# Softmax over 2048 keys with a maximum for each half: one running maximum replaced by two local ones in an attention kernel

## What is computed

```python
logits = jnp.einsum('bhid,bhjd->bhij', q, k) * SCALE
logits = jnp.einsum('bhij,gh->bgij', logits, Wpre)
attn = jax.nn.softmax(logits, axis=-1)
attn = jnp.einsum('bhij,gh->bgij', attn, Wpost)
out = jnp.einsum('bhij,bhjd->bhid', attn, v)
```

## Time and profile before

| | us |
|---|---|
| median of 3 runs | 9106.78 (9100.24 to 9108.23) |
| the profiled execution, its own time | 9105.46 |
| its span in the trace | 9103.7 |
| TensorE busy | 8367.6 (92%) |
| VectorE busy | 8179.9 (90%) |
| ScalarE busy | 7239.7 (80%) |
| GpSimd busy | 5882.0 (65%) |

### The profile page before, as it was taken

The page is one execution under the profiler, slowest core; times in us unless marked ns, Lnnn a source line. Parts: engine busy times, 40 slices in busy tenths (PEclk is TensorE's granted clock), DMA queues, the critical chain, the costliest instruction groups (busy, mean ns, idle before and its releaser), DMA issues.

```text
span 9103.7 us, 399510 instructions
## 1 busy us (share of the span) xinstructions
PE 8367.6 (92%) x158060; PEld 4657.2 (51%) x158060; DVE 8179.9 (90%) x12269; ACT 7239.7 (80%) x13696; POOL 5882.0 (65%) x12005
## 2 busy tenths in 40 slices
PE   7999999997799999999779999999977999999997
PEld 3555555554455555555445555555544555555554
DVE  7999999996899999999689999999968999999996
ACT  5888888885588888888558888888845888888884
POOL 5666666663566676667356667666636666766663
PEclk9999999998899999999889999999989999999998
DMA  0000000002000000000100000000020000000002
GB/s 30 7 8 9 8 8 8 9 8 68 21 7 8 8 9 7 8 8 9 67 21 8 8 8 9 8 8 8 9 67 21 8 8 8 9 8 8 8 9 76
DMA packets 100978, 143.32 MB, mean 16 GB/s; under 512 B 8097, under 2 KB 90657, under 8 KB 96801
## 3 DMA queue, kind: packets, MB, share of 16 engines
q1 hardware_dynamic: 99104, 117.57, 3.9%
HBM read 75.60 MB, written 41.94 MB: 13 GB/s over the span
## 4 chain that ended last, share of the span: by engine, by line
DVE 43%; PE 32%; issue 19%; DVEq 2%; ACT 1%; SPq 1%; DMA 1%; POOL 0%; POOLq 0%; ACTq 0%
PE psS L1172 16%; DVE top L814 14%; DVE big L828 13%; DVE pl L854 9%; PE psP L1192 6%; PE psO L1207 6%; PE psM L1218 1%; DVE top L820 1%; ACT big L642 1%; DVE rr L846 1%; PE psS L1305 1%; PE psS L1147 1%; PE psS L1334 1%; DVEq L813 0%; DMA d_ct<-cT 0%
## 5 line engine op out<-in xcount | busy, mean ns | idle before, releaser
L828 DVE SCALAR_TENSOR_TENSOR big<-psP,big 128x512 f16<-128x512 f32 x4096 | 2608.7, 676 | 289.8 <-ACT big L642 280.7
L814 DVE TENSOR_REDUCE top<-psS 128x1 f32<-128x1024 f32 x2048 | 2482.5, 1212 | 224.1 <-PE psS L1172 223.7
L642 ACT ACTIVATE big<-psP 128x512 f16<-128x512 f32 x4096 | 2199.5, 589 | 581.9 <-PE psP L1192 576.0
L1172 PE MATMUL psS<-KH,AH 128*128 128x512 f16 x8192 | 2466.1, 383 | 81.8 <-POOL AL L440 80.0
L1172 PE MATMUL psS<-KH,AL 128*128 128x512 f16 x8192 | 2441.9, 380 | 0.0
L1172 PE MATMUL psS<-KL,AH 128*128 128x512 f16 x8192 | 2441.3, 380 | 0.0
L624 ACT ACTIVATE pr<-psS,nb 128x1024 f32<-128x1024 f32 x2048 | 2281.4, 1114 | 69.9 <-ACT nb L611 3.9
L652 ACT ACTIVATE ph<-pr 128x1024 f16<-128x1024 f32 x2048 | 2151.8, 1051 | 32.3
L1192 PEld LDWEIGHTS psP<-rh,ph 64*128 64x128 f16 x32768 | 1433.9, 95 | 1221.8 <-DVE big L828 1037.8
L1192 PE MATMUL psP<-rh,ph 64*128 64x64 f16 x32768 | 1682.6, 192 | 383.0 <-DVE big L828 345.6
L854 DVE TENSOR_TENSOR pl<-pr,ph 128x1024 f16<-128x1024 f32 (+1 forms) x2048 | 2024.3, 988 | 0.0
(11 more groups left out here) (138 smaller groups left out, 8004.7 us busy)
## 6 DMA issues: line engine op xcount, KB each, us to landing
ph<-in_xT SPq DMA_DIRECT2D x16, 512.0 KB, 4.4
xr<-in_x SPq DMA_DIRECT2D x64, 128.0 KB, 2.1
d_x<-x SPq DMA_DIRECT2D x64, 128.0 KB, 1.7
d_xn<-xn SPq DMA_DIRECT2D x64, 128.0 KB, 1.7
d_lg<-lg SPq DMA_DIRECT2D x64, 128.0 KB, 1.7
d_ct<-cT SPq DMA_DIRECT2D x64, 128.0 KB, 1.7
Q<-in_w SPq DMA_DIRECT2D x8, 1024.0 KB, 12.2
out<-V SPq DMA_DIRECT2D x16, 512.0 KB, 3.3
```

Source lines behind the costliest of these rows:

```text
L642: a.activation(PT[:, hf * JH:(hf + 1) * JH, :, 0, i0:i0 + HQ], psP[:, ih, :].rearrange("p (j g i) -> p j g i", j=JH, g=H), ACT.Copy, scale ...
L814: v.tensor_reduce(top[:, t % 2, h:h + 1], psS[:, 2 * h:2 * h + 2, :].rearrange("p c n -> p (c n)"), X, ALU.max).then_inc(s_mx, 1)
L828: v.scalar_tensor_tensor(out=PT[:, js, :, 1, i0:i0 + HQ], in0=psP[:, ih, :].rearrange("p (j g i) -> p j g i", j=JH, g=H), scalar=MDROP, in ...
L1172: mm = pe.matmul(psS[:, c, :], A_[:, k8, k, :], K_[:, k, c * CW:(c + 1) * CW], start=n == 0, stop=n == 5)
```

## The change

Each half is now exponentiated with its own maximum, so half 1 no longer needs the maximum of half 0. `row_bound` is gone from VectorE. GpSimd works out nm, the smaller of the two negated maxima (`lower_bound`); ScalarE makes two factors from it, ff = exp(nm - nb) for each half, in the place where it made f0; GpSimd weighs both sums with them (ws), adds them (tot), and after VectorE's reciprocal (now rc) multiplies both factors by it (rr). On GpSimd, `total` also stands behind `mixq` now, with `lower_bound` in its old place.

```diff
+                def lower_bound(T, t):
+                    p = t % 2
+                    g.wait_ge(s_nb, T * 2 + 2 + 1)
+                    apart(g)
+                    g.tensor_scalar(nm[:, p:p + 1], nb[:, p, 0:1], nb[:, p, 1:2], None, ALU.min).then_inc(s_nm, 1)
...
                 def total(T, t):
                     g.wait_ge(s_exp, T * 2 + 2 + 1)
                     g.wait_ge(s_f, T + 1 + 1)
-                    g.tensor_scalar(tot[:, p:p + 1], sums[:, p, 0:1], f0[:, p:p + 1], sums[:, p, 1:2],
-                                    ALU.mult, ALU.add).then_inc(s_tot, 1)
-                def first_half(T, t):
+                    g.tensor_tensor(ws[:, p, :], sums[:, p, :], ff[:, p, :], ALU.mult).then_inc(s_ws, 1)
+                    g.wait_ge(s_ws, T + 1 + 1)
+                    g.tensor_tensor(tot[:, p:p + 1], ws[:, p, 0:1], ws[:, p, 1:2], ALU.add).then_inc(s_tot, 1)
+                def weights(T, t):
                     g.wait_ge(s_rec, T + 1 + 1)
-                    g.tensor_tensor(rr[:, p, 0:1], rr[:, p, 1:2], f0[:, p:p + 1], ALU.mult).then_inc(s_r0, 1)
+                    g.tensor_tensor(rr[:, p, :], ff[:, p, :], rc[:, p:p + 1].broadcast_to([P, 2]), ALU.mult)\
+                     .then_inc(s_r0, 1)
...
                     if one:
-                        total(T - 1, t_1)
+                        lower_bound(T - 1, t_1)
                     if live:
                         mixq(it, t + LEAD, first and t + LEAD < TG)
+                    if one:
+                        total(T - 1, t_1)
                     roots(t, work, 0)
                     if one:
-                        first_half(T - 1, t_1)
+                        weights(T - 1, t_1)
...
                 def bound(T, t, h):
-                    m = 2 * h
-                    a.wait_ge(s_mx, T * 3 + 2 * h + 1 + 1)
-                    a.activation(nb[:, p, h:h + 1], top[:, p, m:m + 1], ACT.Copy, bias=LIFT * math.log(2.0),
+                    a.wait_ge(s_mx, T * 2 + h + 1 + 1)
+                    a.activation(nb[:, p, h:h + 1], top[:, p, h:h + 1], ACT.Copy, bias=LIFT * math.log(2.0),
                                  scale=-SSCALE).then_inc(s_nb, 1)
...
                 def factor(T, t, early):
+                    a.wait_ge(s_nm, T + 1 + 1)
                     if not early:
                         a.wait_ge(s_r0, T - 2 + 1 + 1)
-                    a.activation(f0[:, p:p + 1], nb[:, p, 0:1], ACT.Exp, bias=nb[:, p, 1:2], scale=-1.0).then_inc(s_f, 1)
+                    a.activation(ff[:, p, :], nb[:, p, :], ACT.Exp, bias=nm[:, p:p + 1], scale=-1.0).then_inc(s_f, 1)
...
-                def row_bound(T, t):
-                    v.wait_ge(s_mx, T * 3 + 2 + 1)
-                    v.tensor_tensor(top[:, t % 2, 2:3], top[:, t % 2, 0:1], top[:, t % 2, 1:2], ALU.max).then_inc(s_mx, 1)
...
                     p = t % 2
                     v.wait_ge(s_tot, T + 1 + 1)
-                    v.reciprocal(rr[:, p, 1:2], tot[:, p:p + 1]).then_inc(s_rec, 1)
+                    v.reciprocal(rc[:, p:p + 1], tot[:, p:p + 1]).then_inc(s_rec, 1)
...
                     if live:
                         half_max(T, t, 1)
-                        row_bound(T, t)
```

More of the change, by code:

```diff
@@ L126, in seq_layer @@
         ones = sb("ones", [P, P])
-        top = sb("top", [P, 2, 3])
+        top = sb("top", [P, 2, 2])
         nb = sb("nb", [P, 2, 2])
         sums = sb("sums", [P, 2, 2])
-        f0 = sb("f0", [P, 2])
+        nm = sb("nm", [P, 2])
+        ff = sb("ff", [P, 2, 2])
+        ws = sb("ws", [P, 2, 2])
+        rc = sb("rc", [P, 2])
         tot = sb("tot", [P, 2])
@@ L227, in seq_layer @@
         s_nb = sem("s_nb")
+        s_nm = sem("s_nm")
+        s_ws = sem("s_ws")
         s_f = sem("s_f")
@@ L268, in seq_layer @@
         s_out = sem("s_out")
-        FROM_ONE = [s_A, s_nb, s_f, s_tot, s_rec, s_r0, s_rp, s_rh, s_rl, s_pl, s_plg, s_D, s_F, s_y, s_mx, s_exp, s_ph,
+        FROM_ONE = [s_A, s_nb, s_nm, s_ws, s_f, s_tot, s_rec, s_r0, s_rp, s_rh, s_rl, s_pl, s_plg, s_D, s_F, s_y, s_mx, s_exp, s_ph,
                     s_mh, s_ml, s_oc, s_CTc, s_t1, s_xb, s_st, s_nw]
@@ L504, in total @@
                     g.wait_ge(s_f, T + 1 + 1)
-                    apart(g)
-                    g.tensor_scalar(tot[:, p:p + 1], sums[:, p, 0:1], f0[:, p:p + 1], sums[:, p, 1:2],
-                                    ALU.mult, ALU.add).then_inc(s_tot, 1)
-                def first_half(T, t):
+                    g.tensor_tensor(ws[:, p, :], sums[:, p, :], ff[:, p, :], ALU.mult).then_inc(s_ws, 1)
+                    g.wait_ge(s_ws, T + 1 + 1)
+                    g.tensor_tensor(tot[:, p:p + 1], ws[:, p, 0:1], ws[:, p, 1:2], ALU.add).then_inc(s_tot, 1)
+                def weights(T, t):
                     p = t % 2
                     g.wait_ge(s_rec, T + 1 + 1)
-                    g.tensor_tensor(rr[:, p, 0:1], rr[:, p, 1:2], f0[:, p:p + 1], ALU.mult).then_inc(s_r0, 1)
+                    g.tensor_tensor(rr[:, p, :], ff[:, p, :], rc[:, p:p + 1].broadcast_to([P, 2]), ALU.mult)\
+                     .then_inc(s_r0, 1)
                 def post(T, t):
```

## The result

The changed kernel takes 9029.7 us (9023.8 to 9052.7, 4 runs) against 9105.4 (4 runs) for the kernel before: a ratio of 0.9922, interval 0.9904 to 0.9940. It is 76 us faster. The forecast was 8870, a gain of 237; the time lies on the very edge of the range, and a third of the forecast gain has come.

The account below looks back on a forecast made before the run. A loop through VectorE and GpSimd, closed by L820, was taken as the bound. TensorE 123.3, ordinary slots 1.8, square roots 1.0 and layer norm 0.5 made 126.6 us a block against 130.3: 237 us gained, 8870, range 8710 to 9030.

Parts of the forecast that it names:

- The bound: Attention loop: GpSimd's L497 holds VectorE's L820, closing a loop of 8.0 us a slot through both engines.
- The removal: VectorE without L820: its next work begins about 1.0 us earlier, ScalarE's nb 1.05, until other engines bound the slot.
- idle time and layer norm: Block charges: 1.8 us of idle TensorE in ordinary slots, 0.5 for VectorE's layer-norm steps.
- the 1.0 for the square roots: ScalarE's factor waiting for a late GpSimd in slots with square-root steps: 1.0 us a block.
- 12 ordinary slots at 7.2 us each: Attention slots after the change: three engines at 7.05 to 7.1 overlap imperfectly, so 7.2, with 0.15 of idle TensorE each.
- The range: Whole kernel: 8710 to 9030; the forecast case, chance 0.59, took gaps of 0.0 to 0.35 us a slot as 8760 to 8960.
- lower_bound and factor: GpSimd's nm takes 0.2 us in idle time; the factor's wait costs nothing in ordinary slots, 1.0 us a block at square roots.
- The queries ahead of the total: GpSimd's queries (0.76 us) move into idle time ahead of the factor; total and recip end about where they did.
- Total in two steps: GpSimd: two instructions of 0.2 us with a 0.21 hop replace one of 0.76, mostly blocked by VectorE's low.
- GpSimd sets the pace and most of the gain is lost: Rival, 0.18: GpSimd's slot of 6.4 us, up to 7.6 if low holds the queries; 9074, or 8960 with 7.35.
- The factor's wait closes a new loop: Rival, 0.10: ScalarE's factor waits for nm, nm for L497; slower if GpSimd's slot exceeds 7.8 us, 9490 or 9300.
- What would show it: Trace signs: factor waits on nm only in square-root slots, L497 7.1 to 7.3 us apart in ordinary stretches, L828 0.64 to 0.68.

Follow-up runs that it names:

- e2: The kernel before, with L820 kept but its second maximum given as a scalar operand, one tensor input from SBUF instead of two: 8964.6 us, ratio 0.9846.
- e1: The kernel before with L820 (row_bound) alone taken out, nothing added or moved, no overflow guard: 8858.3 us, ratio 0.9730.
- e7: e1 with nm added at the head of GpSimd's slot and nobody waiting for it: 8874.0 us, ratio 0.9747.
- e6: e1 with nm added at the head of GpSimd's slot and ScalarE's factor waiting for it: 9052.6 us, ratio 0.9947.
- e8: e1 with total moved behind mixq, nothing else: 8926.7 us, ratio 0.9806.
- e3: The changed kernel with total put back ahead of mixq, behind lower_bound: 9101.7 us, ratio 0.9995.
- e5: e1 with GpSimd's total in two instructions, a product and a sum, in place of one: 8852.3 us, ratio 0.9723.
- e13: e6 without the arithmetic of GpSimd's square-root steps, their waits and counts kept: 8852.8 us, ratio 0.9722.
- e14: e7 without the arithmetic of GpSimd's square-root steps, their waits and counts kept: 8844.8 us, ratio 0.9716.

## Why the prediction missed

**The bound was read rightly for most slots.** L820 was held by L497, and e2 shows it with nothing else changed; e1 shows what the loop through both engines was worth. It was not the period of every slot, for behind tiles 4, 11 and 12 e1 is no faster than before.

**The removal** was put at 4.7 us a block after idle time and layer norm, without the 1.0 for the square roots: 123.3 + 1.8 + 0.5 against 130.3, so 301 us. It measured 246 (e1), 3.8 a block. A fifth too much. I had put 12 ordinary slots at 7.2 us each; in e1 they lie between 6.6 and 8.2, and what keeps the long ones long no run shows. The range had a slip as well: a gap of 0.35 us in 12 slots gives 9022 by the prediction's own sum, and not 8960.

**lower_bound and factor is the step that failed.** I charged 1.0 us a block for "the slots with square-root steps", and the wait costs 179 / 64 = 2.8 (e7 to e6). The mechanism, the price of one stand (1.5 us, measured 1.1 to 1.5) and the slots were right. The cover was not. Of the four slots I let the output slot and the one behind it go free, and cut the other pair from 3.0 us to 1.0, "covered by the earlier recip". Only the output slot (tile 10) is free; tiles 6 and 7 stand for 1.52 and 1.33 us in e6 and tile 11 for 1.12, 4.0 us a block, of which 2.8 are paid. Much of each stand is a square-root step that VectorE's low holds for about 1 us, and these holds are in no term of the sum. The instruction itself, put at 0.2 us and hidden, is 0.28 unheld and costs 16 us (e7). There was a row nearer to it than the ones I took: L506 in the earlier trace rows, 0.34, is almost its shortest, 0.33.

**The queries ahead of the total** I charged with nothing, since "total and recip end about where they did". I looked at the slots in which GpSimd idles and not at the two in which it does not. There the cover fails as the next sentence of the prediction feared ("a recip late by 0.3 us holds VectorE by as much"), by 0.43 and 0.81 us. On e1 the move costs 68 us (e8); behind nm it gains 72 (e3). The parts do not add: e1 8858, with nm and its wait 9053, and with the two-step total, the wider factors and the moved queries 9030. In the changed kernel's own context the queries' move was a repair of what nm had broken.

**Total in two steps**: nothing on e1 (e5), as charged. But from e6 (9053) to e3 (9102), which differ in it and in the two-column factors, it is 49 us. Recip's waits for tot in tiles 6, 7 and 11 grow with it, from 50 to 101 us, which fits a longer total that is paid where GpSimd is late. But nm is also held in tile 14 in 52 blocks of e3 and in 8 of e6, and the distances behind tiles 13 and 14 grow by 0.41 and 0.35 us. The two shares are not separated.

**The rivals.** "GpSimd sets the pace and most of the gain is lost" (0.18) is what happened in its result, 9030 against its 8960 to 9074. In its reason only half: GpSimd's chain is not long in every slot; it is late in three of sixteen, and the factor's wait hands that to ScalarE, as recip's wait for tot hands it to VectorE. "The factor's wait closes a new loop" had the mechanism, with a price far too high. The Trainium skill's rule (SBUF — State Buffer, "Who interferes with whom") is that a VectorE instruction with two SBUF inputs contends with a GpSimd one that reads SBUF, and that one with at most one SBUF input, outside the two-port modes, does not. The traces agree: every nm over 0.5 us in the changed kernel (177 of them) ends within 0.16 us of the end of a VectorE low, and L838 is never over 0.70 us. The order of starts in the rows does not tell who is held: in the slot shown nm's row starts 0.12 us before low's. Read by the longest row alone, the held nm would be the culprit, since nm is held in three tiles of the changed kernel; by e13 against e14 that hold, in the one tile where it stands in e6, is worth some 8 us. But the lock also stands one step earlier, on the square-root steps that make nm late, and what it is worth there the runs do not separate from the steps themselves.

**What would show it.** Most signs came as written: L838 unheld at 0.68 us, the factor's waits not in most slots, L864 of 1024 columns grown from 1.21 to 1.28 us on average. Two did not: the factor also waits in tiles 1 and 14, which have no square-root steps, and the distance between lows outside the output slots runs from 6.9 to 8.9 us and not from 7.1 to 7.3. Recip waits for tot in 41 of 222 slots, far from "most", but these are tiles 6, 7 and 11 of each block, and around them the lost time lies. A wait in a few slots of a block had no price in my list.

## What to carry to other kernels

An engine that idles ahead of a wait can take more work, but not a new wait of somebody else on it: the idle time is an average, and the new waiter pays in the slots where the engine is late. Count, slot by slot, how far the engine is ahead at the new wait, with each of its instructions at its held length and not its free one. And before moving work into idle time, find the slots that have none: there the moved work delays what stands behind it, and e8 paid its 68 us in two slots of sixteen.

## What the runs showed of the hardware

- The same maximum of two one-number columns on VectorE is 158 to 1145 ns with two tensor inputs, by what GpSimd does, and 211 to 217 ns in 1024 executions with the second column as a scalar operand. Its free length is longer, 214 against 158; it is held in none of them.
- GpSimd instructions on one or two numbers are held as long as large ones: nm up to 1.40 us beside 0.28, and a square-root step 1.08 beside 0.19, ending 0.05 to 0.15 us behind a low of VectorE. In 71 of the 177 executions of nm over 0.5 us the row of nm starts before that of the low that it ends with.
